# First group's patches from row loads and TensorE transposes, later groups from shifted rows on 128 partitions

## What is computed

```python
patches = _patchify(x, 16)                       # [32, 36, 768], a patch is (channel, row, column)
proj = einsum('bnf,df->bnd', patches, W) + b     # d = 256
h = concat([cls, proj], 1) + pos_enc             # 37 rows
h = concat([h, txt], 1)                          # 114 tokens
y = _layernorm(h); h = h + y + attention(y)      # 16 heads of 64, causal
z = _layernorm(h); h = h + experts(z)            # top 2 of 8, capacity 570, gelu MLP 256-1024-256
```

## Time and profile before

| | us |
|---|---|
| median of 3 runs | 888.43 (887.7 to 889.6) |
| the profiled execution's own time | 888.15 |
| its span | 886.4 |
| TensorE busy | 841.6 (95%) |
| VectorE busy | 563.8 (64%) |
| ScalarE busy | 508.7 (57%) |
| GpSimd busy | 375.0 (42%) |

### The profile page before, as it was taken

How to read it: one execution, slowest core, us unless ns; L and a number is a source line. 1 busy time by engine, 2 the same in 40 slices (tenths; PEclk the granted TensorE clock), 3 DMA queues, 4 the chain that set the end, 5 groups by cost and what they waited for, 6 DMA issues and landing times.

```text
span 886.4 us, 20329 instructions
## 1 busy us (share of the span) xinstructions
PE 841.6 (95%) x7103; PEld 763.1 (86%) x7103; DVE 563.8 (64%) x2458; ACT 508.7 (57%) x1688; POOL 375.0 (42%) x678
## 2 busy tenths in 40 slices
PE   6799999999999999999999999999579999999996
PEld 6688898888889889888888988988569999999995
DVE  3567438566674855866576486477557877668771
ACT  3477657556674765666467377566055555556551
POOL 2144334254543724544364373465614223441334
PEclk9999999999999999999999999999779999999999
DMA  8333120011003102101200110010446444543322
GB/s 237 100 101 153 44 56 23 2 52 49 24 14 78 33 1 68 44 13 36 60 18 2 38 30 6 9 33 3 122 127 194 110 128 115 126 134 96 69 27 28
DMA packets 55575, 57.69 MB, mean 65 GB/s; under 512 B 26831, under 2 KB 47579, under 8 KB 55360
## 3 DMA queue, kind: packets, MB, share of 16 engines
q1 hardware_dynamic: 34834, 45.15, 16.4%
q0 software_dynamic: 18944, 9.76, 6.9%
q10 hardware_dynamic: 1696, 1.49, 0.6%
HBM read 34.25 MB, written 21.89 MB: 63 GB/s over the span
## 4 chain that ended last, share of the span: by engine, by line
PE 80%; DVE 11%; issue 3%; SPq 2%; DMA 1%; ACT 1%; POOL 1%; POOLq 0%; DVEq 0%
PE bank L409 14%; PE bank L411 14%; PE bank L410 14%; PE o_bank L1324 5%; PE score_bank L1304 5%; PE pT_bank L1313 5%; PE bank L1192 3%; DVE sm L1021 2%; PE o_bank L410 2%; PE o_bank L411 2%; PE o_bank L409 2%; PE score_bank L409 2%; PE score_bank L410 2%; PE score_bank L411 2%; PE bank L1274 1%
## 5 line engine op out<-in xcount | busy, mean ns | idle before, releaser
L598 POOL TENSOR_SCALAR pr<-pr,rc 114x114 f32<-114x114 f32 x512 | 181.0, 370 | 300.9 <-DVE rc L1063 299.8
L740 ACT ACTIVATE pr<-sm,nb 114x114 f32<-114x114 f32 x512 | 192.3, 383 | 7.8 <-DVE nb L1025 7.6
L629 POOL DMA_INDIRECT out_dram<-yout,dest x40 | 74.1, 1852 | 159.9 <-ACT yout L786 158.4
L1021 DVE CUSTOM_DVE_ANT_0 sm<-score_bank,mask 114x114 f32<-114x114 f32 x512 | 109.9, 272 | 49.8 <-PE score_bank L1304 49.7
L409 PE MATMUL bank<-xT_hi,wqkv_hi 128*128 128x456 f32 (+1 forms) x288 | 110.8, 385 | 3.0 <-ACT vv L649 1.7
L734 ACT ACTIVATE pT<-pT_bank 114x456 f32<-114x456 f32 x128 | 70.5, 551 | 53.3 <-PE pT_bank L1313 52.8
L410 PE MATMUL bank<-xT_lo,wqkv_hi 128*128 128x456 f32 (+1 forms) x288 | 100.2, 348 | 0.0
L411 PE MATMUL bank<-xT_hi,wqkv_lo 128*128 128x456 f32 (+1 forms) x288 | 100.1, 348 | 0.0
L740 ACT ACTIVATION_READ_ACCUMULATOR pr<-sm,nb 114x1 f32 x512 | 99.0, 193 | 0.0
L713 ACT ACTIVATE oT_hi<-o_bank 128x228 fp32r<-128x228 f32 x128 | 45.3, 354 | 79.2 <-PE o_bank L1324 69.1
L1313 PE MATMUL pT_bank<-ident,pr 114*114 114x114 f32 x512 | 74.3, 267 | 0.7 <-ACT pT L734 0.7
(11 more groups left out here) (203 smaller groups left out, 2254.7 us busy)
## 6 DMA issues: line engine op xcount, KB each, us to landing
stage_a<-in_L_ffn_w_dram SPq DMA_DIRECT2D x8, 1024.0 KB
stage_b<-in_L_ffn_w_dram SPq DMA_DIRECT2D x8, 1024.0 KB
slots_dram<-fill SPq DMA_DIRECT2D x8, 605.6 KB
pix<-in_x_dram SPq DMA_DIRECT2D x96, 36.0 KB, 2.2
xs<-slots_dram SPq DMA_DIRECT2D x8, 363.4 KB
hraw<-in_txt_dram SPq DMA_DIRECT2D x8, 308.0 KB
out_dram<-h SPq DMA_DIRECT2D x8, 308.0 KB
xs<-slots_dram SPq DMA_DIRECT2D x8, 242.2 KB
```

The source lines that it names most:

```text
L598: p = pool.tensor_scalar(pr[:, m % 4, i, :], pr[:, m % 4, i, :], rc[:, m % 4, i:i + 1], 1.0, ALU.mult, ALU.mult)
L629: pool.indirect_dma_start(out, bass.IndirectOffsetOnAxis(ap=dest[e % 2][:, t:t + 1], axis=0), yout[:, t, :], None, compute_op=ALU.add).the ...
L740: a = act.activation(pr[:, N % 4, i, :], sm[:, N % 2, i, :], ACT.Exp, bias=nb[:, N % 2, i:i + 1], scale=SCALE, accum_out=rs[:, N % 4, i:i ...
L1021: m = dve.tensor_tensor_reduce(sm[:, N % 2, i, :], score_bank[i % 2][0:T, o:o + T], mask[:, :], 1.0, NEG, ALU.add, ALU.max, mx[:, N % 2, i ...
```

## The change

Three things are different.

Group 0: one DMA loads `first_raw`, 72 partitions (image, channel, patch row) of 16 whole pixel rows, 6144 bytes each. ScalarE and VectorE reorder one half each into `first_pix`, TensorE transposes it in 12 pieces (jobs P0), and the two engines drain these into `tok`. The weight is transposed in three jobs W0 to `first_W` for this layout. `embed_first` makes 12 products. A second set of transposes (jobs W, from `tok_turned`, which the two engines reorder from `tok_raw`) makes `embW` for the later groups. Normalising, the transposes to `xT` and the first value projections go by pairs of images; the weight splits go in halves of 512 columns. The class row comes as a 37th column of `embT` that is zero, with `base` holding class token and position; GpSimd's queue issues the four DMAs for it.

Groups 1 to 7: a patch's elements lie as 128 partitions times 6 products: partition 16h+r holds row r shifted by 2h columns, and the products go over 3 channels and 2 columns. `load_pixels(g, i)` brings half a group (2 images) by one DMA of 221 KB into partitions 0 to 15, waits for it, and then issues seven copies on the chip, from partitions 0 to 15 to 16h to 16h+15, 221 KB each. `pix` holds half a group, so the next half's load waits for the pack of this one. Packs are two per group, of 432 elements in each partition, at steps 5 and 11. `embed` has 12 matmuls.

Order: group 1 is embedded at step 4 of group 0 instead of in the prologue; its packs stand in ScalarE's queue between the two key drains of the prologue, and at step 2. `clear_slots` moves behind the pixel loads of group 0.

```diff
         LAG_T, LAG_O = 3, 5
         AT_O, AT_V2, AT_E, AT_Y, AT_L, AT_X, AT_M = 4, 5, 6, 10, 11, 13, 13
-        AT_PACK, AT_RSTD1, AT_RSTD2 = 4, 10, 8
+        AT_PACK, AT_RSTD1, AT_RSTD2 = (5, 11), 10, 8
+        AT_FIRST_M = 4
...
+        def embed_at(g, n):
+
+            return [g + 2] * (n == AT_M and g + 2 < G) + [1] * (g == 0 and n == AT_FIRST_M)
+
+        def packed_units(g, i):
+
+            return 2 * (g - 1) + i + 1
...
-            def load_pixels(g):
-
-
-                for b in range(GB):
-                    for c in range(CH):
...
-                    end = (i + 1) * half - HPX
-                    start = 0 if i == 0 else half - HPX
-                    sp.dma_start(flat[1:2 * PR:2, start:end], flat[0:2 * PR:2, start + HPX:end + HPX]).then_inc(pix_in, 16)
+            def rows_of_images(b):
+
+                return x[b:b + 2].rearrange("b c (n r) w -> r (b c n) w", r=PX)
+
+            def load_pixels(g, i):
+
+                if (g, i) != (1, 0):
+                    sp.wait_ge(packed, packed_units(g, i) - 1)
+                sp.dma_start(pix[0:PX, :].rearrange("r (n w) -> r n w", w=IMG), rows_of_images(GB * g + 2 * i)).then_inc(rows_in, 16)
+                sp.wait_ge(rows_in, 16 * packed_units(g, i))
+                for h in range(1, SH):
+
+                    sp.dma_start(pix[PX * h:PX * (h + 1), 0:PIX - JJ * h], pix[0:PX, JJ * h:PIX]).then_inc(pix_in, 16)
...
+            sp.dma_start(first_raw[:, :], x[0:GB].rearrange("b c (n r) w -> (b c n) (r w)", r=PX)).then_inc(first_in, 16)
             sp.dma_start(tok_raw[:, :, :], tokW.rearrange("(c p) f -> p c f", p=128)).then_inc(tokW_in, 16)
...
+            load_pixels(1, 0)
             sp.dma_start(stage_d[:, :].rearrange("p (c n) -> p c n", c=HP), Wo.rearrange("(c p) n -> p c n", p=128)).then_inc(wo_in, 16)
...
-            sp.wait_ge(packed, 1)
-            load_pixels(1)
+            load_pixels(1, 1)
...
-            sp.wait_ge(packed, 2)
-            load_pixels(2)
...
+                    load_pixels(2, 0)
+                if g + 2 < G:
+                    load_pixels(g + 2, 1)
                 if g > 0:
                     wait_all(sp, drained("O", 2 * g - 1))
                     set_out(g - 1)
+                if g + 3 < G:
+                    load_pixels(g + 3, 0)
+                if g == 0:
+                    clear_slots()
...
+            def pack(g, i):
+
+                act.wait_ge(pix_in, 16 * (SH - 1) * packed_units(g, i))
+                act.wait_ge(filled, job_filled("M", g - 1))
+                dst, src = patches(pix, slice(0, 128), i, slice(0, 128), 0)
...
+            act.wait_ge(first_in, 16)
+            act.activation(*first_patches(0), ACT.Copy).then_inc(first_packed[0], 1)
+            act.dma_start(stage_a[:, :].rearrange("p (c n) -> p c n", c=KC), Wv.rearrange("(c p) n -> p c n", p=128)).then_inc(wv_in, 16)
+            drain_weights("W0", 1, first_W)
+            drain_patches(0)
+            act.wait_ge(tokW_in, 16)
+            dst, src = turned_weights(0)
+            for c in range(CH):
+                t = act.activation(dst[:, c], src[:, c], ACT.Copy)
+            t.then_inc(turned[0], 1)
+            split_columns(2 * HD, 0, stage_a, wv_in, wv_hi)
+            for k in range(JS // 2):
+                drain_weights("W", k, embW)
+            split_columns(HD, 0, stage_c, wk_in, wk_hi)
+            drain_first_x(0)
+            split_columns(0, 0, stage_b, wq_in, wq_hi)
+            drain_v(0, 0)
+            drain_v(0, 1)
+            drain_first_x(1)
+            split_columns(HD, 1, stage_c, wk_in, wk_hi)
+            split_columns(2 * HD, 1, stage_a, wv_in, wv_hi)
+            drain_v(0, 2)
+            split_columns(0, 1, stage_b, wq_in, wq_hi)
+            drain_v(0, 3)
+            split_high(wo_hi[:, :, :], stage_d[:, :].rearrange("p (c n) -> p c n", c=HP), wo_in, wo_hi_done)
             drain_k(0)
+            pack(1, 0)
             drain_k(1)
...
             def drain_embedded(g):
-                drain("M", g, embT[:, :, :], job_bank("M", g)[:, 0:KC * GB * NP].rearrange("p (k t) -> p k t", k=KC))
+                for k in range(KC):
+                    src = job_bank("M", g)[:, k * GB * NP:(k + 1) * GB * NP].rearrange("p (b n) -> p b n", b=GB)
+                    if k == 0:
+                        dve.wait_ge(filled, job_filled("M", g))
+                    m = dve.tensor_copy(embT[:, k, :, 0:NP], src)
...
+            dve.wait_ge(first_in, 16)
+            dve.tensor_copy(*first_patches(1)).then_inc(first_packed[1], 1)
+            for k in (0, 2):
+                drain_weights("W0", k, first_W)
+            drain_patches(1)
+            dve.wait_ge(tokW_in, 16)
...
+            split_columns(2 * HD, 0, stage_a, wv_hi, wv_lo)
+            dve.wait_ge(base_made, 1)
+            first_statistics(0)
+            first_statistics(1)
+            first_normalise(0)
+            drain_first_x(0)
+            first_normalise(1)
+            split_columns(HD, 0, stage_c, wk_hi, wk_lo)
+            drain_first_x(1)
+            split_columns(0, 0, stage_b, wq_hi, wq_lo)
+            split_columns(HD, 1, stage_c, wk_hi, wk_lo)
+            split_columns(2 * HD, 1, stage_a, wv_hi, wv_lo)
+            drain_q(0)
+            split_columns(0, 1, stage_b, wq_hi, wq_lo)
...
 
-                pe.wait_ge(packed, g + 1)
+                pe.wait_ge(packed, packed_units(g, 1))
+                wait_all(pe, drained("W", JS // 2 - 1))
                 dst = claim("M", g)
                 for k in range(KC):
-                    for j in range(HPX):
-                        m = pe.matmul(dst[:, k * GB * NP:(k + 1) * GB * NP], embW[:, j, k * 128:(k + 1) * 128], tok[:, j, :],
-                                      start=(j == 0), stop=(j == HPX - 1))
+                    for j in range(JS):
+                        m = pe.matmul(dst[:, k * GB * NP:(k + 1) * GB * NP], embW[:, j, k * 128:(k + 1) * 128], tok[:, j % JJ, :, j // JJ, :],
+                                      start=(j == 0), stop=(j == JS - 1))
+                m.then_inc(filled, 1)
...
+            def embed_first():
+
+                for k in range(JS // 2):
+                    wait_all(pe, drained("W0", k))
+                for h in range(2):
+                    wait_all(pe, drained("P0", h))
+                dst = claim("M", 0)
+                for k in range(KC):
+                    for h in range(2):
+                        for c in range(CH):
+                            m = pe.matmul(dst[:, k * GB * NP:(k + 1) * GB * NP], first_W[:, 2 * c + h, k * 128:(k + 1) * 128],
+                                          first_tokens(h)[:, c * GB * NP:(c + 1) * GB * NP], start=(h + c == 0), stop=(h + c == CH))
                 m.then_inc(filled, 1)
...
+            for k in range(JS // 2):
+                transpose_weights("W0", k, lambda dc, j: tok_raw[:, dc, 128 * j:128 * (j + 1)])
+            for h in range(2):
+                dst = claim("P0", h)
+                pe.wait_ge(first_packed[h], 1)
+                for m_ in range(NPS):
+                    m = pe.transpose(dst[:, m_ * FIRST:(m_ + 1) * FIRST], first_pix[:, h, m_, :], ident[0:FIRST, 0:FIRST])
                 m.then_inc(filled, 1)
-            stay_warm(16)
-            wait_all(pe, drained("W", 3))
-            embed(0)
+            embed_first()
             transpose_patches(0)
-            stay_warm(16)
-            transpose_tokens("X", 0, xn, xn_done)
-            tokens_split(0)
-            pe.wait_ge(wv_lo, 1)
-            for b in range(GB):
+            for done in turned:
+                pe.wait_ge(done, 1)
+            for k in range(JS // 2):
+                transpose_weights("W", k, lambda dc, j: tok_turned[:, dc, j, :])
+            stay_warm(6)
+            transpose_first_tokens(0)
+            for b in range(2):
                 project_v(0, b, 0)
-            pe.wait_ge(wk_lo, 1)
+            transpose_first_tokens(1)
+            for b in range(2, GB):
+                project_v(0, b, 0)
             project("K", 0)
-            pe.wait_ge(wq_lo, 1)
             project("Q", 0)
             project("K", 1)
-            embed(1)
```

More of the change, by code:

```diff
@@ new lines, in _, with rstd, dispatch @@
+            pool.wait_ge(consts_done, 1)
+            def rstd(k, vareps, done, ve, out_t, images=slice(0, GB)):
+                pool.wait_ge(vareps, k + 1)
+                pool.tensor_tensor(out_t[:, images], ve[:, images], neg_half[:, images], ALU.pow).then_inc(done, 1)
+            def dispatch(v, i):
+                after((routed, routed_after(v, 5)), (slots_cleared, 16 * (E + 1)))
+                b, j = divmod(i, TOPK)
+                b += unit_images(v)[0]
+                slots_of = slot if v < LAST else slot_last
+                pool.indirect_dma_start(slots, bass.IndirectOffsetOnAxis(ap=slots_of[:, j, b:b + 1], axis=0),
+                                        rows[unit_group(v) % 2][:, b, :], None, bounds_check=E * CAP - 1, oob_is_err=False).then_inc(dispatched, 16)
```

(34 more changed lines are left out.)

260 lines of the change are left out of this document (124 added, 136 removed).

## The result

The changed kernel takes **923.6 us** (median of 4 runs, 922.7 to 925.8) against 888.5 for the kernel before on the same chip: ratio 1.040, 95% interval 1.038 to 1.042. The forecast was 878.6, range 873 to 906: wrong in sign, and outside the range. Rival 1 had the mechanism, and was 20 us too cheap.

What follows compares the result with a forecast made beforehand. TensorE was taken to bound the steps, and a chain over all engines the prologue. 888.15 - 7.7 (prologue) + 2.9 (group 1's embedding) + 1.1 (step-4 wait) - 5.8 (six embeddings) = 878.6 us, range 873 to 906.

Steps and rivals of the forecast that it cites:

- Rival 1: On-chip copies are bound by their 16 source partitions, slower: C = 15 gives 903 us, 18.8 gives 918; chance 40%.
- C: Time of the seven on-chip copies in one pixel round: 6.3 us assumed at 246 GB/s, ends 6.3 and 18.8.
- The low end, 82 GB/s: Copy rate if a transfer's rate goes with its partitions, 246 x 16/48, making C 18.8 us.
- break-even: Copy rate where the chain costs as much as the change gains: C = 11.4, 136 GB/s; below that, slower.
- 1.1: TensorE's new wait at step 4 of group 0, for group 1's pixels to be packed: 1.1 us.
- 7.1 + C: Length of one pixel round in us: load issue and landing, first copy's issue, seven copies C, completion, pack.
- A: When ScalarE has packed group 1's first half, so the second half can load: 36.2 us, 39.9 with C = 15.
- `clear_slots` is wanted in group 2 only: Clearing the slots, behind group 0's pixel loads, is not needed before group 2; no cost was summed for it.
- The prologue, -7.7: First masking comes at 39.0 us instead of 46.70, 7.7 us less; bounds 4 to 10 less.
- the 17.6 in the sum: Prologue: time in us of the next transpose after the first embedding, 1.7 ahead of the old 19.31.
- 5.8 in six: Embeddings of groups 2 to 7 in the steps: 24 records instead of 32, 0.96 us less each, 5.8 in all.
- +2.9: Group 1's embedding moves from the prologue into the steps of group 0, adding 2.9 us there.

Runs made afterwards that it cites:

- spread layout: Changed kernel with the 16 source rows of the seven copies at partitions 0, 8, ... 120 instead of 0 to 15, weight layout matched: 886.3 us, ratio 0.998.
- e8_all: e4_direct with Wo's low split moved into steps 1 and 3, Wv loaded first, group 1's pixels issued behind Wo, Wv's low split behind the statistics: 885.0 us, ratio 0.996.
- e4_direct: Direct loads: changed kernel with eight shifted loads from DRAM per half group, in the spread layout, instead of on-chip copies: 885.8 us, ratio 0.998.
- e10_step5: e8_all with group 1's embedding at step 5 instead of 4 and ScalarE's packs in group 0 at steps 3 and 6: 881.6 us, ratio 0.994.
- e11_warm: e10_step5 with nine idle products instead of six ahead of the first X transposes: 879.1 us, ratio 0.991.

## Why the prediction was wrong

**The step that failed** is the size of C: "I take 6.3, since the trace shows the engines as what limits a copy, and nothing that shows a partition limit." Measured: 1.545 MB at 112 GB/s, 13.8 us. The row behind it read 246 GB/s at a DMA share of 0.82, and I took the share for a limit. After, the share is 1.06 at 112 GB/s, and 1.08 at 221 in the spread layout: it reads the same at half the rate, so it can't tell an engine at its limit from one that is held up elsewhere. (Rival 1 had this wrong too: it expected a share near 0.3.) The low end, 82 GB/s, scaled with the number of partitions; the spread layout refutes that too. The prediction's own break-even was 136 GB/s, and the measured rate is under it, so by its own sum the kernel had to be slower. The 104 GB/s that the prediction quoted from the Trainium skill ("SBUF — State Buffer", section "Door 1: The DMA port swizzle") and left out of its sum was within 8% of the measured rate.

How much of the miss is C? The spread layout copies at 221 GB/s, which makes C 7.0, close to the 6.3 assumed, and it took 886.3 us. So of the 45.0 us between forecast and result 37.3 are C's, and 7.7 are not: there the first masking was at 42.72 and not 39.0, TensorE waited 4.4 us (3.0 and 1.4) for ScalarE in group 0 and not 1.1, and group 1's embedding ran partly at the lower clock (4.14 us).

**The form of the sum was right, its inputs late.** A round is 7.1 + C = 20.9 with C measured, 22.0 in the trace. But the first half was packed at 46.55, where the sum had A at 36.2 (39.9 in rival 1): the rows landed at 22.4, not 16.7, and Wo stood behind seven copies on SyncE and landed at 44.3. SyncE's issues take 1.6 us each (11.22 for seven), not 0.57: with transfers backed up the issue itself is held. In place of 1.1 us TensorE waited 11.7 at step 4, 6.5 at step 8, and 5.1 for Wo at the prologue's end; part of its work behind these ran at the lower clock.

**Rival 1's 903 lacked two things**: those 6.7 us of A, with the waits and lower clock behind them (group 2 at 117.7, not 107.2, 10.5), and group 1, where the lag grew by 8.8 although one embedding became 1.0 cheaper, so 9.8, and where "`clear_slots` is wanted in group 2 only" looked at who waits for the clearing, not at what stands behind it. 903 + 10.5 + 9.8 = 923.3, against 925.8 in the profiled execution: 2.5 us stay unexplained.

**The prologue, -7.7.** In the changed kernel the first masking was at 49.08, later than the old 46.70, since VectorE's split of Wo waited for Wo behind the copies. That is C's doing. By the run without copies masking comes at 42.25, not 39.0: 4.5 us earlier than the earlier trace rows, within the bounds of 4 to 10. `xn` came at 24.39 in the changed kernel, not 22.2, although the way back to tokens began at 17.11, ahead of the 17.6 in the sum. VectorE's rows say why; the half split of Wv waited for ScalarE's, that for Wv, and the tokens stood behind it:

```profile
19.40 1.22 DVE L878 TENSOR_TENSOR wqkv_lo<-stage_a,wqkv_hi 128x1024 fp32r<-128x1024 f32 x1 [2.34 <-ACT wqkv_hi L722]
20.54 0.68 DVE L954 TENSOR_TENSOR hraw<-bank,base 37x512 f32<-37x512 f32 x1
```

The sum followed the data's chain and not VectorE's queue. With the order mended in `e8_all` `xn` came 5.7 us behind the way back (16.95 to 22.69) in place of 7.3. The value projections of the first two images ran at the lower clock in the changed kernel (0.50 from 22 to 32 us), which the sum had assumed away.

**What was right**: 24 records in 3.12 us at the upper clock, 0.96 us less per embedding, 5.8 in six; the extra copies and packs on VectorE and ScalarE hidden; +2.9 for group 1's embedding in the steps, where the clock was at its upper level (2.86 us to the next matmul with direct loads). With spread rows or direct loads and the order of the prologue and the steps mended, the kernel comes to 879.1, on a chip where the kernel before takes 2 us less than where the forecast was made; the ratio, 0.991, is close to the forecast's 0.989. That is chance as much as the sum: it took moves which the forecast did not have.

Open: which side of a copy, source or destination, sets its rate; why the direct loads keep the share above 1 (1.12 at 166 GB/s from 50 to 60 us), whether by their 328-byte pieces or by the destination; why the first embedding takes 3.2 us in some traces and 4.6 to 5.2 in others; and how much of the 30.9 us is waiting and how much the lower clock behind it.

## What to carry to other kernels

When a change moves data between partitions on the chip, ask where its source and destination lie before asking how many bytes: a band of 16 adjacent partitions halved the rate, and spreading the same rows cost nothing here. A DMA share near one is not proof that the DMA engines are the limit. And for every wait that goes or comes, walk the queue of the engine that holds it: ScalarE's pack, SyncE's clearing and VectorE's weight split each delayed something that had nothing to do with them.

## What the runs showed of the hardware

- Copies within the chip: 112 GB/s from partitions 0 to 15 to another 16 adjacent ones, 221 from 0, 8, ... 120 to 16 spread alike, 221 from 0 to 31, 220 from 0 to 63, with the DMA share between 1.05 and 1.08 in each.
- SyncE's issue of one DMA took 0.57 us with free queues, 0.84 in the spread layout (5.87 for seven), 1.6 with the slow copies, and 12.93 for one text load behind the clearing. In these runs transfers that back up hold the engine that issues.
- The granted clock fell to its lower level after TensorE's waits of 4 to 12 us, and also behind smaller gaps: in the changed kernel's prologue after 2.66 and 1.27 us, in `e4_direct` some 2 us behind a wait of 1.77, in `e8_all` and `e10_step5` in a stretch with gaps of 1.27, 0.89 and 1.10 us. In `e11_warm`, with 0.22 in place of 0.89, it stayed at the upper level (1.00 up to 60 us); that is one trace.
